# One-pass fp32r projections from split operands in an attention block, with reordered engine queues

## The reference

```python
emb = silu(_sin_emb(timestep)) @ W_ada + b_ada
x = _ln(src) * (1.0 + scale) + shift            # 32 sequences of 256 tokens, 256 features
q = (x @ Wq + bq); k = (x @ Wk + bk); v = (x @ Wv + bv)      # 16 heads of 16
scores = q k^T / 4 + attention_bias; masked with -inf; probs = softmax(scores)
x = x + (ctx @ Wo + bo)
x = x + gelu2(_ln(x) * g2 + beta2 @ W1 + b1) @ W2 + b2        # 1024 hidden
# then U (256 x 32), V (256 x 32) are orthonormalised column by column and
# x + strength * response(x) is returned
```

## Time and profile before

| | |
|---|---|
| median of 3 runs | 1373.11 us (1371.91 to 1373.67) |
| the profiled execution | 1371.87 us, its span 1369.7 us |
| busy share of the span, PE / DVE / ACT / POOL | 96% / 79% / 78% / 64% |
| busy share from 300 to 900 us, PE / DVE / ACT / POOL | 97% / 77% / 84% / 87% |
| batches 1 to 31 start (first to last) | 38.45 to 826.44 us |
| phase 2, first product | 900.98 us |
| granted TensorE clock, mean | 0.989 of full speed (2.4 GHz) |

### The profile page before, as it was taken

The page is one execution under the profiler, slowest core; times in us unless marked ns, Lnnn a source line. Parts: engine busy times, 40 slices in busy tenths (PEclk is TensorE's granted clock), DMA queues, the critical chain, the costliest instruction groups (busy, mean ns, idle before and its releaser), DMA issues. The chain is left out here.

```text
span 1369.7 us, 39618 instructions
## 1 busy us (share of the span) xinstructions
PE 1317.9 (96%) x11934; PEld 1117.0 (82%) x11934; DVE 1076.0 (79%) x3635; ACT 1071.3 (78%) x2664; POOL 870.5 (64%) x874
## 2 busy tenths in 40 slices
PE   3899999999999999999999998889999999999997
PEld 3677777777777777777777776579999999999997
DVE  3787777887777778787777778568888888888885
ACT  0788888888888888888888887777777777777773
POOL 3989999998998999999899898321222222122210
PEclk9999999999999999999999999989999999999998
DMA  7656565564655656556466582101011010101100
GB/s 233 213 168 197 166 200 169 179 209 147 203 183 168 200 165 193 177 171 211 151 197 191 159 272 70 32 24 40 31 46 31 31 46 31 46 31 40 37 24 32
DMA packets 182894, 175.07 MB, mean 128 GB/s; under 512 B 15776, under 2 KB 182336, under 8 KB 182848
## 3 DMA queue, kind: packets, MB, share of 16 engines
q1 hardware_dynamic: 182848, 174.49, 40.4%
HBM read 157.69 MB, written 16.78 MB: 127 GB/s over the span
## 5 line engine op out<-in xcount | busy, mean ns | idle before, releaser
L423 POOL TENSOR_TENSOR ring<-ring,maskv 128x1024 f32<-128x1024 f32 x256 | 600.1, 2373 | 13.7 <-DMA ring<-in_fside 6.4
L899 ACT ACTIVATE ring<-ring,nmax 128x256 f32<-128x256 f32 x1024 | 452.6, 501 | 29.0 <-DVE nmax L599 28.9
L599 DVE CUSTOM_DVE_ANT_0 ring<-bank,ring 128x256 f32<-128x256 f32 x1024 | 373.1, 418 | 90.9 <-PE bank L1158 74.5
L904 ACT ACTIVATE pT<-bank 128x512 f32<-128x512 f32 x416 | 239.4, 592 | 100.9 <-PE bank L1173 100.9
L1173 PE MATMUL bank<-ident,ring 128*128 128x128 f32 x2048 | 293.0, 279 | 1.4 <-ACT pT L904 1.1
L1173 PEld LDWEIGHTS bank<-ident,ring 128*128 128x128 f32 x2048 | 232.1, 143 | 70.9 <-issue 47.9
L1034 ACT ACTIVATE work<-bank,b1t 128x256 f32<-128x256 f32 x256 | 107.4, 475 | 109.2 <-PE bank L1369 109.2
L1158 PE MATMUL bank<-work 32*128 32x256 f32 x2048 | 148.2, 403 | 5.2 <-DVE nmax L599 5.2
L1369 PE MATMUL bank<-hT_high,w_high 128*128 128x256 f32 x512 | 147.9, 289 | 3.5 <-DVE hT_rest L771 3.5
L1382 PE MATMUL bank<-w_high,gT_high 128*128 128x256 f32 x512 | 148.2, 289 | 0.0
L1382 PE MATMUL bank<-w_high,gT_rest 128*128 128x256 f32 x512 | 145.2, 284 | 0.0
(11 more groups left out here) (158 smaller groups left out, 2723.5 us busy)
## 6 DMA issues: line engine op xcount, KB each, us to landing
ring<-in_fside SPq DMA_DIRECT2D x128, 1024.0 KB, 7.6
xt<-in_x SPq DMA_DIRECT2D x32, 256.0 KB, 3.2
x_d<-x2s SPq DMA_DIRECT2D x32, 256.0 KB, 7.8
work<-x_d SPq DMA_DIRECT2D x32, 256.0 KB, 2.7
out<-pT SPq DMA_DIRECT2D x32, 256.0 KB, 2.2
mk<-in_mask SPq DMA_DIRECT2D x32, 64.0 KB, 6.7
w<-in_W SPq DMA_DIRECT2D x2, 1024.0 KB, 10.5
wada<-in_W_ada SPq DMA_DIRECT2D x1, 512.0 KB, 4.2
```

Of the source, the lines that this page charges most:

```text
L423: nc.gpsimd.tensor_tensor(v, v, m, ALU.add).then_inc(s_masked, 1)
L599: nc.vector.tensor_tensor_reduce(out=v, in0=score_ps[h % HG][:, qt], in1=v, scale=-1.0, scalar=ROW_MAX_NEG, op0=ALU.add, op1=ALU.min, accu ...
L899: nc.scalar.activation(v, v, ACT.Exp, bias=nmax[:, b.par, h, qt:qt + 1], scale=-1.0).then_inc(s_exp, 1)
L904: nc.scalar.activation(pT[:, h % (2 * HG)], tp_ps[h % 2], ACT.Copy).then_inc(s_pta, 1)
```

## The change

The six raw weight tiles and `wada` now lie in `pT`, which is free until the first head; in their place come `wqs`, `wks`, `wvs`, `wos`, a `high` and a `rest` tile each, filled in the set-up by ACT and DVE. `xT_out` writes back into `prep_ps`; ACT's new `xT_high` and DVE's new `xT_rest` make the two parts `xTs`; likewise `ctxT_out` and `ctxT_rest` for `ctxTs`. The four projections are three fp32r products for one. `x_back` is 8 products with an fp32r identity in place of 4 transposes. Three small POOL steps are dropped or merged, and one (adding the epsilon to the norm) goes to DVE. The queues of PE, DVE and ACT are reordered. DMAs are the same in number and order. ACT's order in the loop becomes: exp 2, copy 15 (b-1), xT_high, copy 0, exp 3, exp 4, pv_out 3 (b-1), copy 1, copy 2, exp 5, gs_coefficients, exp 6, copy 4, copy 5, exp 7 to 11, pv_out 0, copy 6, gs_write, gs_column, ctxT_out, copy 8, 9, 10, exp 12, 13, pv_out 1, exp 14, 15, copy 12, exp 0 (b+1), copy 13, exp 1 (b+1), copy 14, pv_out 2. `pv(b, 1)` waits for `ctxT_rest` where it waited for ctxT_out.

```diff
-    nc.gpsimd.tensor_tensor(nrm[:], gii[:], expo[:, 1], ALU.pow).then_inc(s_gp, 1)
-    pool.wait_ge(s_gp, i + 2)
-    pool.nop(nofuse=True)
-    nc.gpsimd.tensor_scalar(nrme[:], nrm[:], GS_EPS, 1.0, ALU.add, ALU.mult).then_inc(s_gnrm, 1)
+    nc.gpsimd.tensor_tensor(nrm[:], gii[:], expo[:, 1], ALU.pow).then_inc(s_gnrm, 1)
 def gs_update(i):
     pool.wait_ge(s_gcoef, i + 1)
     pool.nop(nofuse=True)
-    for a in range(2):
-        for c in range(DC):
-            ins = nc.gpsimd.tensor_scalar(gprod[:, a, c], coef[:, a], qcol[:, a, c:c + 1], 1.0, ALU.mult, ALU.mult)
-    ins.then_inc(s_gprod, 1)
+    nc.gpsimd.tensor_tensor(gprod[:], coef[:].unsqueeze(2).to_broadcast([P, 2, DC, R]), qcol[:].unsqueeze(3).to_broadcast([P, 2, DC, R]),
+                            ALU.mult).then_inc(s_gprod, 1)
     pool.wait_ge(s_gprod, i + 1)
...
     pool.nop(nofuse=True)
     nc.gpsimd.tensor_scalar(vpe[:], mv[:, :, 1], LN_EPS, 1.0, ALU.add, ALU.mult)
-    nc.gpsimd.tensor_scalar(mneg[:], mv[:, :, 0], -1.0, 1.0, ALU.mult, ALU.mult).then_inc(s_pool, 1)
-    pool.wait_ge(s_pool, 2 * b.n + 1)
-    nc.gpsimd.tensor_tensor(rstd[:], vpe[:], expo[:, 0], ALU.pow).then_inc(s_pool, 1)
-    pool.wait_ge(s_pool, 2 * b.n + 2)
-    nc.gpsimd.tensor_tensor(nmr[:], mneg[:], rstd[:], ALU.mult).then_inc(s_rstd, 1)
+    nc.gpsimd.tensor_scalar(mean[:], mv[:, :, 0], 1.0, 1.0, ALU.mult, ALU.mult).then_inc(s_pool, 1)
+    pool.wait_ge(s_pool, b.n + 1)
+    nc.gpsimd.tensor_tensor(rstd[:], vpe[:], expo[:, 0], ALU.pow).then_inc(s_rstd, 1)
...
     for t in range(QT):
-        ins = nc.gpsimd.tensor_scalar(xn[:, t], xt[:, b.par, t], rstd[:, t:t + 1], nmr[:, t:t + 1], ALU.mult, ALU.add)
+        ins = nc.gpsimd.tensor_scalar(xn[:, t], xt[:, b.par, t], mean[:, t:t + 1], rstd[:, t:t + 1], ALU.subtract, ALU.mult)
     ins.then_inc(s_xn, 1)
...
 def stats(b):
     dve.wait_ge(s_x[b.par], 16 * b.half + 16)
+    if b.i is not None or b.off >= 1:
+        dve.wait_ge(s_stats, b.n)
+        dve.nop(nofuse=True)
...
-    nc.vector.tensor_copy(by_head[:, :, a], by_dim[:, :, a])
+    ins = nc.vector.tensor_copy(by_head[:, :, a], by_dim[:, :, a])
+ins.then_inc(s_wp, 1)
+def weight_rest(i):
+    (high, rest), w = ((wqs, wqp), (wks, wkp), (wvs, wv), (wos, wo))[i]
+    dve.wait_ge(s_wh, i + 1)
+    nc.vector.tensor_tensor(rest[:], w, f32(high[:]), ALU.subtract).then_inc(s_wl, 1)
+for i in range(4):
+    weight_rest(i)
+dve.wait_ge(s_const, 1)
+nc.vector.tensor_copy(identr[:], ident[:])
 nc.vector.memset(pooled[:], 0.0).then_inc(s_setup, 1)
...
 def gs_reciprocal(i):
     dve.wait_ge(s_gnrm, i + 1)
+    nc.vector.tensor_scalar(nrme[:], nrm[:], GS_EPS, None, ALU.add).then_inc(s_geps, 1)
+    dve.wait_ge(s_geps, i + 1)
     nc.vector.reciprocal(rnrm[:], nrme[:]).then_inc(s_grec, 1)
...
     dve.wait_ge(s_xtp, b.n + 1)
     for c in range(DC):
-        ins = nc.vector.tensor_scalar(xT[:, c], prep_ps[:, c], adaS[:, c, bass.ds(b.n, 1)], adaB[:, c, bass.ds(b.n, 1)], ALU.mult, ALU.add)
+        ins = nc.vector.tensor_scalar(prep_ps[:, c], prep_ps[:, c], adaS[:, c, bass.ds(b.n, 1)], adaB[:, c, bass.ds(b.n, 1)], ALU.mult, ALU.add)
     ins.then_inc(s_xT, 1)
+def xT_rest(b):
+    dve.wait_ge(s_xh, b.n + 1)
+    if b.i is not None or b.off >= 1:
+        dve.wait_ge(s_vp, b.n)
+    nc.vector.tensor_tensor(xTs[1][:], prep_ps, f32(xTs[0][:]), ALU.subtract).then_inc(s_xl, 1)
+def ctxT_rest(b):
+    dve.wait_ge(s_ctxT, b.n + 1)
+    nc.vector.tensor_tensor(ctxTs[1][:], tail_ps, f32(ctxTs[0][:]), ALU.subtract).then_inc(s_cl, 1)
 def q_out(b, a):
-    if a == 0:
-        dve.wait_ge(s_qp, b.n + 1)
+    dve.wait_ge(s_qp, b.n + 1)
     ins = nc.vector.scalar_tensor_tensor(qm[:, b.par, a], prep_ps, half[:, a:a + 1], bqm[:, a].unsqueeze(2).to_broadcast([P, DC, S]),
                                          ALU.mult, ALU.add)
...
+    if main:
+        reduces(b, (0, 1))
     if n is None or n >= 2:
         x2_out(b.plus(-2))
     if main:
+        reduce_head(b, 2)
         xres_out(b)
-        if n is None or 1 <= n < B - 2:
-            stats_end(b.plus(2))
         reduce_head(b, 3)
     if prep:
         xT_out(b.plus(1))
-    if main:
-        reduce_head(b, 4)
+        xT_rest(b.plus(1))
+    if main:
+        reduces(b, (4, 5, 6))
+    if prep:
+        q_out(b.plus(1), 0)
+    if main:
+        reduce_head(b, 7)
     if tail:
         gs_reciprocal(b.plus(-1).n)
     if main:
-        reduces(b, (5, 6, 7))
         copy_pT(b, 3)
     if n == 0:
         stats(Batch(2))
         stats_end(Batch(2))
+    if n is None or 1 <= n < B - 2:
+        stats_end(b.plus(2))
     if n == B:
         stats2(Batch(1))
+    if tail:
+        normalise_ctx(b.plus(-1), 0)
     if prep:
-        q_out(b.plus(1), 0)
         q_out(b.plus(1), 1)
-    if tail:
-        normalise_ctx(b.plus(-1), 0)
+    if n is None or n + 3 < B:
+        stats(b.plus(3))
+    if tail:
+        normalise_ctx(b.plus(-1), 1)
     if main:
         reduce_head(b, 8)
-    if tail:
-        normalise_ctx(b.plus(-1), 1)
-    if main:
-        reduce_head(b, 9)
     if prep:
         k_out(b.plus(1))
     if main:
-        reduce_head(b, 10)
-        copy_pT(b, 7)
-        reduce_head(b, 11)
...
         v_out(b.plus(1))
     if n == B - 2:
         constants2()
     if main:
-        reduces(b, (12, 13, 14, 15))
+        copy_pT(b, 7)
+        reduces(b, (12, 13))
+    if tail:
+        ctxT_rest(b.plus(-1))
+    if main:
+        reduces(b, (14, 15))
         gs_products(b)
-        if n is None or n + 3 < B:
-            stats(b.plus(3))
         copy_pT(b, 11)
-    if prep:
-        reduces(b.plus(1), (0, 1, 2))
     if n == B:
         response_matrix(0)
...
 def ctxT_out(b):
     act.wait_ge(s_cT, b.n + 1)
-    nc.scalar.activation(ctxT[:], tail_ps, ACT.Copy).then_inc(s_ctxT, 1)
+    nc.scalar.activation(ctxTs[0][:], tail_ps, ACT.Copy).then_inc(s_ctxT, 1)
+def xT_high(b):
+    act.wait_ge(s_xT, b.n + 1)
+    if b.i is not None or b.off >= 1:
+        act.wait_ge(s_vp, b.n)
+    nc.scalar.activation(xTs[0][:], prep_ps, ACT.Copy).then_inc(s_xh, 1)
 def column(i):
...
+for i, ((high, rest), w) in enumerate(((wqs, wqp), (wks, wkp), (wvs, wv), (wos, wo))):
+    if i < 2:
+        act.wait_ge(s_wp, i + 1)
+    if i == 2:
+        act.wait_ge(s_load_att, 16 * len(loads_att))
+    nc.scalar.activation(high[:], w, ACT.Copy).then_inc(s_wh, 1)
...
 def project_qk(b, t):
-    w = wqp if t == 0 else wkp
+    ws = wqs if t == 0 else wks
     if t == 0:
-        pe.wait_ge(s_xT, b.n + 1)
+        pe.wait_ge(s_xl, b.n + 1)
     else:
         pe.wait_ge(s_qev, b.n + 1)
     for n in range(DC):
         for c in range(DC):
-            ins = mm(prep_ps[:, n], w[:, c, n * P:(n + 1) * P], xT[:, c], start=(c == 0), stop=(c == DC - 1))
+            for k, (kw, kx) in enumerate(HI_LO):
+                ins = mm(prep_ps[:, n], ws[kw][:, c, n * P:(n + 1) * P], xTs[kx][:, c],
+                         start=(c == 0 and k == 0), stop=(c == DC - 1 and k == len(HI_LO) - 1))
     ins.then_inc(s_qp if t == 0 else s_kp, 1)
 def project_v(b):
     pe.wait_ge(s_kev, b.n + 1)
     for t in range(QT):
         for c in range(DC):
-            ins = mm(prep_ps[:, t], xT[:, c, t * P:(t + 1) * P], wv[:, c], start=(c == 0), stop=(c == DC - 1))
+            for k, (kx, kw) in enumerate(HI_LO):
+                ins = mm(prep_ps[:, t], xTs[kx][:, c, t * P:(t + 1) * P], wvs[kw][:, c],
+                         start=(c == 0 and k == 0), stop=(c == DC - 1 and k == len(HI_LO) - 1))
     ins.then_inc(s_vp, 1)
...
     for t in range(QT):
         for c in range(DC):
-            ins = nc.tensor.transpose(prep_ps[:, t, c * P:(c + 1) * P], xT[:, c, t * P:(t + 1) * P], ident[:])
+            for k in range(2):
+                ins = mm(prep_ps[:, t, c * P:(c + 1) * P], xTs[k][:, c, t * P:(t + 1) * P], identr[:], start=(k == 0), stop=(k == 1))
     ins.then_inc(s_xb, 1)
...
 def project_o(b, main):
-    pe.wait_ge(s_ctxT, b.n + 1)
+    pe.wait_ge(s_cl, b.n + 1)
     if main:
         pe.wait_ge(s_pvc, NG * b.n + NG + 2)
     for t in range(QT):
         for c in range(DC):
-            ins = mm(tail_ps[:, t], ctxT[:, c, t * P:(t + 1) * P], wo[:, c], start=(c == 0), stop=(c == DC - 1))
+            for k, (kx, kw) in enumerate(HI_LO):
+                ins = mm(tail_ps[:, t], ctxTs[kx][:, c, t * P:(t + 1) * P], wos[kw][:, c],
+                         start=(c == 0 and k == 0), stop=(c == DC - 1 and k == len(HI_LO) - 1))
     ins.then_inc(s_o, 1)
...
+    if tail:
+        pv(b.plus(-1), 3)
+    if prep:
+        project_qk(b.plus(1), 0)
+    if main:
         transposes(b, 1)
         transposes(b, 2)
-    if prep:
-        project_qk(b.plus(1), 0)
+    if tail:
+        ctx_natural(b.plus(-1), 0)
     if main:
         transposes(b, 3)
-    if tail:
-        pv(b.plus(-1), 3)
-    if main:
         transposes(b, 4)
+        scores(b, 2)
+    if tail:
+        ctx_natural(b.plus(-1), 1)
+    if main:
         transposes(b, 5)
-    if tail:
-        ctx_natural(b.plus(-1), 0)
```

(46 more changed lines are left out.)

92 lines of the change are left out of this document (44 added, 48 removed).

## The result

The changed kernel takes 1375.0 us, the kernel before 1373.0 in the same comparison (medians of 20 runs each); the ratio is 1.0021, with a 95% interval from 1.0013 to 1.0029. It is slower by 2 us. The forecast was 1366.6, faster by 6.5; its range, 1346 to 1398, holds the time, its likeliest sign does not. The ratio is always to the kernel before, timed beside the run, and counts only runs within 1.5% of the fastest of their kernel, which leaves runs out in b_eps_newxn alone.

A forecast was written before the change was run, and what follows sets the result against it. PE was taken to bound the loop: 26.27 - 1.21 + 0.37 + 0.5 = 25.93 us a period, -10.1 us in 30 periods; with +3.3 at the start and +0.3 at the end, -6.5, so 1366.6 us; 80% range 1346 to 1398.

The forecast's parts named there:

- the paragraph on POOL: POOL's merged gs_update and dropped small steps: with 1.1 us idle waiting for coef, they buy 0.
- the rival of the held step: DVE's epsilon step is held by POOL's additions: 1.18 us a period, +35 us, 1402; chance 0.12.
- The loop without the hold: One period of phase 1's loop: from 26.27 to 25.93 us, -10.1 us over 30 periods.
- Projections: PE's four projections as fp32r products: 1.43 us each in place of 1.73, -1.21 us a period.
- x back: PE's return of x to rows by 8 fp32r products: 0.81 us in place of 0.44, +0.37 a period.
- The rival at float32's pace: x back runs at float32's pace per column: 1.73 us, +27.6 us in all, 1394; chance 0.24.
- The wait for q: PE stands before the q projection until DVE's subtraction for x is done: stall of 0.22 us a period.
- The second context half: PE waits for DVE's normalised context (ctxn) before the second half: stall of 0.3 us a period.
- Set-up: Extra copies and subtractions put s_setup 2.9 us later; with batch 0's chain, +3.3 us in all at the start.
- Phase 2: Left as it is and costed at nothing: it only starts later or earlier as a whole.

The follow-up runs named there:

- b_eps_newxn: The kernel before with the epsilon step moved from POOL to DVE and the new form of xn (subtract mean, multiply by rstd): 1397.3 us, ratio 1.0109.
- eps_pool: The changed kernel with the epsilon step back on POOL: 1354.9 us, ratio 0.9881 to the kernel before.
- xn_old: The changed kernel with x normalised in its old form (multiply by rstd, add nmr): 1356.5 us, ratio 0.9878 to the kernel before.
- a_vpeb: The changed kernel with tile vpeb allocated ahead of xres, putting xres and vt at the addresses of the kernel before: 1380.4 us.
- b_m32: The kernel before with mneg and nmr in one tile, which moves xres and vt down by 32 bytes; no instruction changed: 1364.5 us.

## Why the prediction was wrong

**The step that failed** is the paragraph on POOL, "so this buys nothing by itself: 0", with the argument against the rival of the held step: that POOL's body takes 23.9 us from `coef`, so that the last addition ends at 6.2 us, before the step is issued at 6.6. The body is 25.2. The difference is the new form of xn, 2 x (1.223 - 0.550) = 1.35 us, an edit that stands in the diff and was counted only as two small steps less. (The prediction's 24.07 for the earlier trace rows should read 614.74 + 9.33 - 600.06 = 24.01; nothing hangs on that.) With 25.2 the prediction's own sum gives 8.2 + 25.2 - 25.93 = 7.5 for the end of the addition, well behind the step's 6.6. Measured from the start of the x transposes, the step is issued at 607.08 - 600.55 = 6.5 and the addition ends at 7.25.

The rule of the Trainium skill that the prediction gave for this rival (SBUF — State Buffer, "Who interferes with whom") was borne out: VectorE's `tensor_scalar` blocks fully. That rule has the lock last for one whole instruction; here it could last for more, up to 5.28 us in b_eps_newxn, over two ends of additions, and the measurement decides. The rival's price was off: "+35" took half an addition on the path of each period. The price is 18 us in the 30 periods (793.39 against 775.76 of eps_pool), because the loop locks the step to the last 0.8 us of the addition.

That the range holds 1375 is luck. Against the forecast the loop took 15.5 us more and the start 3.8 more, and phase 2 gave 7.9 back; none of the three causes was in the sum.

**The other terms.**

- *The loop without the hold.* 25.93 was forecast; xn_old has 25.85 and eps_pool 25.86. This sum was right, in part because small misses cancel: the two waits take 0.14 us each in xn_old (617.56 to 617.70 and 596.86 to 597.00) where 0.5 was forecast for both, and PE's groups some 0.1 more than forecast.
- *Projections.* 1.43 us were taken for a group; q takes 605.33 - 603.80 = 1.53. The steps are at 0.119 ((605.21 - 604.02) / 10), as in the earlier trace rows, but the first takes 0.22.
- *x back.* 0.81 was taken, 0.92 measured (624.12 to 625.04), 0.11 a product with 128 columns. The rival at float32's pace (1.73) falls.
- *The wait for q.* 0.22 forecast, 0.20 measured (602.60 + 1.00 to 603.80).
- *The second context half.* 0.3 forecast, 0.73 measured, of which the hold makes about 0.6 (0.76 less the 0.14 that the step was priced at).
- *Set-up.* `s_setup` came 2.7 us later (22.87 - 20.19), forecast 2.9. All of it was to be +3.3, and +7.1 came. The difference is PE's pace: in the changed kernel's profile k, v, x back and the scores of batch 0 run at half pace (scores 2.09 us against 1.15 for the 16 instructions), where k and v did not before. It isn't a fixed part of the change: in eps_pool, with the same set-up, k already runs at full pace and batch 1 starts at 41.53, +3.1, and in xn_old at 45.99. The granted clock does not tell them apart where the pace differs: it reads 1.00 from 25 to 40 us in all three. It reads 0.50 (1.2 GHz) for 6.8 us from 40.0 in eps_pool, and nowhere in the first 100 us in the changed kernel and in xn_old. By batch 3 eps_pool is still 3.6 us ahead of the changed kernel (92.97 against 96.55). What decides between the two starts stays open.
- *Phase 2.* "I cost it at nothing" was wrong by 7.9 us. The change shortened and merged tiles ahead of xres and vt, and most of the gain hangs on 32 bytes of their address.

Taken apart, then: the addresses gave about -8 (-5.4 by a_vpeb), and the rest of the change +10.5 (1375.0 against 1364.5 of b_m32), where without the hold it gives -8 to -10 (xn_old and eps_pool against b_m32).

## What to carry to other kernels

An ALU form is a price of its own: look each changed operation up by its form, also where its shape and engine stay. A small VectorE step from SBUF to SBUF beside a GpSimd engine that is busy most of the time can cost whole microseconds, and if that GpSimd work depends on its result, the two lock and every idle gap that looks like slack is on the path. Before crediting a gain in a stage that wasn't edited, move the tiles of the old kernel to the new addresses.
